# Table products of split queries, the division of local attention, and counts in bf16, in a two-layer attention kernel with an expert layer

## The chip, the cores and the metric

The kernel runs on one core of one Trainium2 chip. The metric is the time of one execution on the device in microseconds, over the whole program. Engines are called TensorE (PE, with PEld for its loads of stationary operands), VectorE (DVE), ScalarE (ACT), GpSimd (POOL) and SyncE (SP), whose queue issues most DMAs.

## The reference

Input x is 8 images of 16x16 positions with 192 channels, in float32. Cut to what matters:

```python
# layer 0: windowed attention (12 heads of 16, windows of 14x14, padded), then an MLP
qkv = win(layer_norm(x)) @ qkv_w + qkv_b
attn = (q * 0.25) @ k.T
rel_h = einsum('bhwc,hkc->bhwk', q, Rh)      # Rh, Rw: tables of relative positions
rel_w = einsum('bhwc,wkc->bhwk', q, Rw)
attn = softmax(attn + rel_h[..., :, None] + rel_w[..., None, :])
x = x + (attn @ v) @ proj_w + proj_b
x = x + gelu(layer_norm(x) @ fc1_w + fc1_b) @ fc2_w + fc2_b
# layer 1: causal attention over the 256 positions (12 heads of 16), then 8 experts, top 2
t = t + causal_attention(ln(t)) @ lin_w.T + lin_b
gates = softmax(ln(t) @ gate_w + gate_b); the two largest, divided by their sum
t = t + sum over the two experts of gate * (gelu(ln(t) @ w1[e] + b1[e]) @ w2[e] + b2[e])
```

## The kernel before

**Stages.** The 8 images go through a pipeline. `run(step)` makes nine steps; in step s, image s is in stage a, image s-1 in b, s-2 in c and s-3 in d (`step(a, b, c, d)`, written out by hand for every engine). Stage a: layer norm, queries, keys and values of local attention (`transpose_a`, `q_a`, `k_a`, `v_a_main`, `v_a_out`) and the table products (`rel_rows`, `rel_columns`). Stage b: local attention itself (`max_a`, `row_a`, `attend_a`, `output_a`) and the MLP (`transpose_m`, `fc1`, `fc2`). Stage c: the second attention (`q_b` to `v_b_all`, `max_b_of`, `row_b`, `attend_b`, `output_b`). Stage d: routing (`gate`, `choose`, `count`, `locate`, `scatter`). After the loop, `last` finishes the second attention of the last image between the first of 39 expert tiles (`tile_transpose`, `tile_fc1`, `tile_fc2`), and a last pass adds the experts' rows. What order instructions have on an engine is that of the code; engines wait for one another by semaphores that count.

**Local attention with tables.** A head pair's queries lie on 128 partitions, head e of the pair on a slot of 64 rows: each slot has 32 rows in which a channel's high and low part go, then 28 rows for the position terms, one for the maximum and three for masks. For each of 16 rows and 16 columns of the image one product, `positions` (L1815 to L1819), multiplies a table `rel_w[:, table, :]` (128 stationary columns) with the queries `s_q` of the 16 positions in that row or column, for six pairs at once: 96 moving columns. The results of the rows are copied by ScalarE (`rel_rows`, L860) into `rel_sum`, those of the columns added by VectorE (`rel_columns`, L1231). Both operands are float32. `s_q` gets its 16 query rows of a slot by a DMA from `staged_a` (L388), and its constant rows once by a DMA.

Four positions make a block of a bank (BANK_A, two halves in turn), so an image has four row blocks and four column blocks; each column block waits for the addition or copy two blocks earlier. After the last, `split_odd`, `split` and `split_even` cut `rel_sum` into a float32r high part and the rest, and the next step's first maxima product waits for that.

**Division.** The value products of four heads (a group, `values_a`) land in BANK_Z with the sum of a head's exponentials in the row behind its 16 channels. `normalise_a` (L1278 to L1284) copies that row over the other rows of its 32 with a shuffle, takes the reciprocal of 128x256 numbers, and multiplies three pieces into `o_a`, from the order of windows into the order of the image. The next group's value products wait for the semaphore `ot_a` of the last piece. The second attention does it otherwise (`normalise_b`, L1344 to L1352): transpose of 32x32 blocks, so that a head's sum lies beside its channels, a reciprocal of 8 columns, one product, and a transpose back.

**Rows of maxima.** Each attention takes the maxima of all heads first, transposes them on TensorE (`row_a`, `row_b`, L2018), has ScalarE copy them, and a DMA puts them into the queries as one row (L401, L422). `attend_a` and `attend_b` wait for that DMA (`row_in_a`, `row_in_b`).

**Counts.** `count` (L2079 to L2081) multiplies a triangle of ones and a square of ones with the choices of the tokens, in float32, with up to 16 moving columns.

## Time and profile before

| | us |
|---|---|
| median of 3 runs | 863.15 |
| the three runs | 858.99, 863.15, 865.65 |
| the profiled execution | 858.26 |
| its span (first to last instruction) | 856.4 |
| mean granted clock of TensorE | 0.933 of full |

The profile is of one execution. Its times are in microseconds from the start of the span. Busy time of TensorE is that of pipelined products with modelled ends, so it is no measure of its peak. The clock is granted at one of two levels, 1.00 being 2.4 GHz and 0.5 being 1.2 GHz; a stretch shows the mean.

### The profile page before, as it was taken

To read this page: it belongs to the slowest core of one execution; us is meant where nothing else is said; L and a number is where in the kernel's file an instruction comes from. 1 tells how busy PE (TensorE), PEld (TensorE's weight loads), DVE (VectorE), ACT (ScalarE), POOL (GpSimd) and SP (SyncE) were. 2 spreads that over 40 slices of the span, in tenths; PEclk is the share of its full clock that TensorE was granted. 3 is DMA by queue.
4 is the path that set the end of the run, shared out by engine and by line. 5 is a ranking of instruction groups with operands and counts; after the bars stand their busy time and mean duration, and the time that the engine had idled before them with its cause. 6 is when DMAs were issued, how large, how long until landed. Compare 5 with 4: busy or idle time off the path is not lost.

```text
span 856.4 us, 15650 instructions
## 1 busy us (share of the span) xinstructions
PE 737.3 (86%) x5694; PEld 647.3 (76%) x5694; DVE 448.4 (52%) x1073; ACT 333.1 (39%) x724; POOL 156.1 (18%) x306
## 2 busy tenths in 40 slices
PE   4688889989989988998998998878688999999990
PEld 3558778868868867886886887757577999999990
DVE  4355656857667683575767768353534222222213
ACT  6124354333433523344353452423273444444430
POOL 5010000121030220113103022012204121211210
PEclk9999999999999996899999998579798999999995
DMA  6702944931030212203012021955304111111117
GB/s 223 176 11 72 250 108 130 226 94 43 24 89 6 67 38 56 57 11 94 23 46 77 19 57 38 238 151 159 111 7 121 43 39 42 44 42 39 43 34 225
DMA packets 62049, 72.18 MB, mean 84 GB/s; under 512 B 6370, under 2 KB 52286, under 8 KB 61846
## 3 DMA queue, kind: packets, MB, share of 16 engines
q1 hardware_dynamic: 58566, 64.17, 27.7%
q0 software_dynamic: 3408, 7.02, 2.7%
q8 instruction: 47, 0.77, 0.4%
q14 instruction: 28, 0.23, 0.1%
HBM read 27.26 MB, written 23.17 MB: 59 GB/s over the span
## 4 chain that ended last, share of the span: by engine, by line
PE 73%; DVE 9%; DMA 6%; issue 5%; ACT 4%; SPq 1%; POOL 1%; another core or an unknown queue 1%; DVEq 0%; POOLq 0%; ACTq 0%
PE ps L2129 8%; PE ps L1819 7%; PE ps L2112 6%; PE ps L2113 6%; PE ps L1777 5%; PE ps L1778 5%; PE ps L1971 4%; PE ps L1944 4%; PE ps L1995 3%; PE ps L1896 3%; PE ps L1910 3%; DVE max_rows_a L1260 2%; PE ps L2034 2%; DMA q_rows_a<-max_at 2%; PE ps L1863 2%
## 5 line engine op out<-in xcount | busy, mean ns | idle before, releaser
L2112 PE MATMUL ps<-rows_t,w_tile 97*128 97x128 f32 x468 | 91.4, 276 | 3.3 <-DVE rows_t L1488 3.3
L2113 PE MATMUL ps<-rows_t,w_tile 96*128 96x128 f32 x468 | 90.5, 274 | 0.0
L2129 PE MATMUL ps<-w_exp,hid_t 128*128 x468 | 84.2, 331 | 2.3 <-DVE y_out L1496 1.4
L1479 DVE COPY w_tile<-w_exp 96x768 f32 x39 | 21.7, 556 | 120.3 <-PE ps L2113 102.1
L1328 DVE TENSOR_REDUCE max_b<-ps 128x3 f32<-128x384 f32 x96 | 48.6, 549 | 68.9 <-PE ps L2012 67.9
L1819 PE MATMUL ps<-s_q,rel_w 128*128 128x96 f32 x512 | 79.5, 314 | 3.0 <-DMA s_q<-staged_a 1.2
L2129 PEld LDWEIGHTS ps<-w_exp,hid_t 128*128 128x128 f32 x468 | 76.4, 193 | 3.5 <-issue 3.5
L1819 PEld LDWEIGHTS ps<-s_q,rel_w 128*128 128x128 f32 x512 | 74.3, 203 | 5.1 <-issue 2.7
L2112 PEld LDWEIGHTS ps<-rows_t,w_tile 97*128 97x128 f32 x468 | 72.4, 191 | 5.2 <-DVE rows_t L1488 5.1
L881 ACT ACTIVATE probs_a<-ps 98x392 f32<-98x392 f32 x96 | 47.9, 499 | 70.1 <-PE ps L1899 68.3
L2113 PEld LDWEIGHTS ps<-rows_t,w_tile 96*128 96x128 f32 x468 | 70.8, 191 | 0.0
L682 POOL DMA_INDIRECT y_dram<-y_out,tile_x x39 | 37.4, 958 | 167.9 <-DVE y_out L1496 167.4
L917 ACT ACTIVATE probs_b<-ps 128x384 f32<-128x384 f32 x96 | 42.2, 488 | 34.3 <-PE ps L2025 33.2
L1896 PE MATMUL ps<-q_rows_a,ks_a 128*98 128x196 f32 x192 | 44.1, 316 | 9.8 <-DMA q_rows_a<-max_at 7.4
L1260 DVE TENSOR_REDUCE max_rows_a<-ps 98x4 f32<-98x784 f32 x48 | 46.3, 965 | 11.6 <-PE ps L1863 9.9
L951 ACT ACTIVATE b_gate<-b,tile_x 128x192 f32 x39 | 17.7, 455 | 82.5 <-DVE y_out L1496 75.2
L941 ACT ACTIVATE hid_t<-ps 128x384 f32<-128x384 f32 x78 | 37.3, 482 | 25.5 <-PE ps L2113 23.5
L1863 PE MATMUL ps<-ks_a,q_rows_a 128*98 128x196 f32 x192 | 31.2, 287 | 18.2 <-DVE max_rows_a L1260 9.6
L1995 PE MATMUL ps<-mask_q,ident 128*128 128x256 bf16 x96 | 30.7, 320 | 18.4 <-issue 11.5
L615 POOL TENSOR_TENSOR x_2b<-x,b_fc 128x384 f32<-128x384 f32 x8 | 8.0, 1003 | 209.0 <-DVE x L1292 209.0
L1863 PEld LDWEIGHTS ps<-ks_a,q_rows_a 128*98 128x98 f32 x192 | 22.9, 176 | 26.7 <-DVE max_rows_a L1260 15.7
L1280 DVE RECIPROCAL den<-den 128x256 f32<-128x256 f32 x24 | 42.1, 1753 | 0.8
(229 smaller groups left out, 1633.0 us busy)
## 6 DMA issues: line engine op xcount, KB each, us to landing
xs_dram<-blank SPq DMA_DIRECT2D x32, 388.0 KB, 8.6
w_exp<-in_e_w SPq DMA_DIRECT2D x16, 576.0 KB
ks_a<-staged_a SPq DMA_DIRECT2D x32, 192.0 KB
qs_b<-staged_b SPq DMA_DIRECT2D x32, 192.0 KB
ks_b<-staged_b SPq DMA_DIRECT2D x32, 192.0 KB
tile_x<-xs_dram SPq DMA_DIRECT2D x39, 97.0 KB
w_exp<-y_dram SPq DMA_DIRECT2D x8, 384.0 KB, 6.7
rel_w<-in_rel_tables SPq DMA_DIRECT2D x1, 1792.0 KB, 9.6
```

Source lines behind the costliest of these rows:

```text
L881: ac.activation(probs_a[0:HALF, p % 3, e, 0:2 * WIN], BANK_W[0:HALF, e, 0:2 * WIN], ACT.Exp)
L1260: dv.tensor_reduce(max_rows_a[0:HALF, 0:2, 2 * p:2 * p + 2].rearrange("p q e -> p e q"), BANK_W[0:HALF, :, 0:2 * WIN].rearrange("p e (q k) ...
L1328: ins = dv.tensor_reduce(max_b3[:, h, :], BANK_C[:, h % 3, 0:384].rearrange("p (a k) -> p a k", a=3), AX.X, ALU.max, negate=True).then_inc ...
L1777: pe.matmul(dst, w[0:DC + ones, 0, cols], x[0:DC + ones, 0, :], start=True, stop=False)
L1778: return pe.matmul(dst, w[0:DC, 1, cols], x[0:DC, 1, :], start=False, stop=True)
L1819: return pe.matmul(dst, rel_w[:, table, :], toks, start=True, stop=True)
L1863: ins = pe.matmul(BANK_W[0:HALF, e, q * WIN:(q + 1) * WIN], qs_a[:, 2 * p + e, q * HALF:(q + 1) * HALF], ks_a[:, 2 * p + e, 0:WIN], start= ...
L1896: pe.matmul(bank[0:HALF, k * WIN:(k + 1) * WIN], ks_a[:, h, k * HALF:(k + 1) * HALF], qs_a[:, h, 0:WIN], start=True, stop=True)
L1995: pe.matmul(bank.rearrange("p (a k) -> p a k", a=2)[:, :, 0:P], ident16[:, :], mask[:, :, :], start=True, stop=False, skip_group_check=True)
L2112: pe.matmul(dst, w1_tile[t % 2][:, 0, cols], rows_t[t % 2][:, 0, :], start=True, stop=False)
L2113: ins = pe.matmul(dst, w1_tile[t % 2][0:DC, 1, cols], rows_t[t % 2][0:DC, 1, :], start=False, stop=True)
L2129: ins = pe.matmul(TILE_Y[:, 0:D], hid_t[t % 2][:, f, :], w_exp[:, bass.ds(e, 1), 2 * MLP + f * D:2 * MLP + (f + 1) * D].rearrange("p e d - ...
```

## The change

- **Table products.** `s_q` and `rel_w` are float32r. Of a slot's 32 rows before the position columns only 16 were used for the queries; now a slot of 64 holds the high part of the queries, their low part, the high part again, and the constants (in rows 48 to 63). The tables have their high part twice, then their low part. So one float32r product per position gives high x high + low x high + high x low. The number of positions and the 96 moving columns stay; each was two float32 instructions and is one now.
- For that VectorE takes the low part of the queries (`low_queries_a`), and SP issues six DMAs an image into `s_q` in place of two. In the first step the raw tables come by 16 DMAs into `probs_a` and `hid`, ScalarE (`tables_set`) and VectorE (`low_tables`) round them and VectorE subtracts the low part, and POOL fills the constant rows of `s_q` (`query_rows_set`).
- **Division of local attention** by blocks transposed, as in the second attention, into `hid`; POOL copies the result into `o_a` (`place_a`). The next group's value products wait for the first transpose (`dn_a`, and `dn_b` in the second attention).
- **Counts** with bf16 operands.
- The hand-written orders of all engines are permuted.

```diff
-            s_q = sb("s_q", [P, PAIRS, TOK])
+            s_q = sb("s_q", [P, PAIRS, TOK], F32R)
...
-        rel_loads = ((s_q[:, :, :], a["slot_rows_q"].unsqueeze(1).to_broadcast([P, PAIRS, TOK])),
-                     (rel_w[:, :, :], a["rel_tables"]))
+        rel_loads = [(q_rows_in, a["slot_rows_q"])]
+        for s in (0, SLOT):
+            for part, tables in zip(raw_tables, TABLES):
+                rel_loads += [(part[s + HD * n:s + HD * (n + 1)], a["rel_tables"][r:r + HD, tables])
+                              for n, r in enumerate((s, s, s, s + SLOT - HD))]
...
             def queries_in_a(i):
...
+                for s in (0, SLOT):
+                    for r in (s, s + 2 * HD):
+                        sp.dma_start(s_q[r:r + HD, :, :].bitcast(F32), staged_a[:, s // SLOT, :]).then_inc(q_in_a, 16)
+                sp.wait_ge(ql_a, i + 1)
+                for s in (0, SLOT):
+                    sp.dma_start(s_q[s + HD:s + 2 * HD, :, :].bitcast(F32), low_q[:, s // SLOT, :]).then_inc(q_in_a, 16)
...
+            def query_rows_set(i):
+                if i == 0:
+                    gp.wait_ge(rel_in, REL_IN)
+                    gp.tensor_copy(s_q[:, :, :], q_rows_in.unsqueeze(1).to_broadcast([P, PAIRS, TOK])
+                                   ).then_inc(constants_set, 1)
...
+            def place_a(g):
+                def go(i):
+                    gp.wait_ge(back_a, GROUPS * i + g + 1)
+                    hold(gp)
+                    for dst, src in zip(window_pieces(yx(o_a[:, g:g + 1, :])), win_order(hid[:, 2 * g + 1:2 * g + 2, :])):
+                        ins = gp.tensor_copy(dst[:, 0], src[:, 0])
+                    ins.then_inc(ot_a, 1)
...
+            def tables_set(i):
+                if i == 0:
+                    ac.wait_ge(rel_in, REL_IN)
+                    ac.copy(rel_w[:, TABLES[0], :], raw_tables[0]).then_inc(rel_set, 1)
...
+            def low_tables(i):
+                if i == 0:
+                    dv.wait_ge(rel_in, REL_IN)
+                    dv.tensor_copy(rel_w[:, TABLES[1], :], raw_tables[1]).then_inc(rel_set, 1)
+                    dv.wait_ge(rel_set, 2)
+                    for s in (0, SLOT):
+                        rows = slice(s + REL, s + REL + HD)
+                        for n, tables in enumerate(TABLES):
+                            cols = slice(s, s + REL + 2 * WS)
+                            part = rel_w[rows, tables, cols]
+                            ins = dv.tensor_tensor(part, raw_tables[n][rows, :, cols],
+                                                   part.bitcast(F32), ALU.subtract)
+                    ins.then_inc(rel_set, 1)
...
+            def low_queries_a(i):
+                dv.wait_ge(qh_a, i + 1)
...
+                dv.tensor_tensor(flat(low_q).bitcast(F32R), BANK_A[0:DC, 1], flat(staged_a[:, 0:2, :]),
+                                 ALU.subtract).then_inc(ql_a, 1)
...
-                    dv.stream_shuffle(den[:, :], src, [HD] * 32).then_inc(dn_a, 1)
+                    dv.transpose(turned, BANK_Z[:, 0:TOK]).then_inc(dn_a, 1)
                     dv.wait_ge(dn_a, done)
-                    dv.reciprocal(den[:, :], den[:, :]).then_inc(rc_a, 1)
+                    dv.reciprocal(sums, blocks[:, :, HD]).then_inc(rc_a, 1)
...
+                    dv.tensor_tensor(blocks[:, :, 0:HD + 1], blocks[:, :, 0:HD + 1],
+                                     sums.unsqueeze(2).to_broadcast([P, TOK // 32, HD + 1]), ALU.mult).then_inc(ml_a, 1)
+                    dv.wait_ge(ml_a, done)
+                    dv.transpose(hid[:, 2 * g + 1, :], turned).then_inc(back_a, 1)
...
             def v_a_main(i):
                 pe.wait_ge(qh_a, i + 1)
+                pe.wait_ge(ql_a, i + 1)
...
-                            pe.wait_ge(ot_a, GROUPS * i + p // 2 - 1)
+                            pe.wait_ge(dn_a, GROUPS * i + p // 2 - 1)
...
-                pe.matmul(counts, before[:, :], both[:, :, :].rearrange("p t e -> p (t e)"), start=True, stop=False)
+                pe.matmul(counts, before16[:, :], both[:, :, :].rearrange("p t e -> p (t e)"), start=True, stop=False)
```

The order of TensorE around the second attention's row of maxima, in a steady step. L1944 is the output product of local attention, L1819 the table products, L2018 and L2019 the transposes of the maxima, L1995 the first product that waits for their DMA. Before (the row block ahead of the output is the third of the image):

```order
L1819 MATMUL ps<-s_q,rel_w 128x96 x8
L1944 MATMUL ps<-w_out_a,o_a 128x192 x6
L1819 MATMUL ps<-s_q,rel_w 128x96 x4
L2018 MATMUL ps<-ident,max_b 12x128
L2019 MATMUL ps<-ident,max_b 12x128
L1819 MATMUL ps<-s_q,rel_w 128x96 x8
L1995 MATMUL ps<-mask_k,ident 128x2x128
```

The same place of TensorE in the changed kernel, where L1898 are the table products, L2023 the output, L2097 and L2098 the transposes and L2074 the product that waits:

```order
L1898 MATMUL ps<-s_q,rel_w 128x96 x4
L2023 MATMUL ps<-w_out_a,o_a 128x192 x6
L2097 MATMUL ps<-ident,max_b 12x128
L2098 MATMUL ps<-ident,max_b 12x128
L1898 MATMUL ps<-s_q,rel_w 128x96 x16
L2074 MATMUL ps<-mask_k,ident 128x2x128
```

Two row blocks moved from ahead of the transposes to behind them, so four blocks (16 products) now stand between the transposes and the product that waits.

VectorE in the first step, from the constants to the first addition of a column block. Before:

```order
L1187 CAST mask_q<-probs_a 128x256
L1188 CAST mask_k<-probs_a 128x256
L1222 SCALAR_TENSOR_TENSOR staged_a<-ps,staged_a 96x512
L1231 TENSOR_TENSOR rel_sum<-ps,rel_sum 128x4x96 x4
L1247 CAST q_rows_a<-rel_sum 64x6x196
```

VectorE in the changed kernel, at the same place (L1270 and L1277 make the tables, L1286 the low queries, L1291 the low keys, L1300 the additions):

```order
L1233 CAST mask_q<-probs_a 128x256
L1234 CAST mask_k<-probs_a 128x256
L1270 CAST rel_w<-hid 128x1536
L1277 TENSOR_TENSOR rel_w<-probs_a,rel_w 16x16x60
L1277 TENSOR_TENSOR rel_w<-hid,rel_w 16x12x60
L1277 TENSOR_TENSOR rel_w<-probs_a,rel_w 16x16x60
L1277 TENSOR_TENSOR rel_w<-hid,rel_w 16x12x60
L1286 TENSOR_TENSOR rel_sum<-ps,staged_a 96x512
L1291 SCALAR_TENSOR_TENSOR staged_a<-ps,staged_a 96x512
L1300 TENSOR_TENSOR rel_sum<-ps,rel_sum 128x4x96 x4
```

Five instructions for the tables and one for the low queries stand ahead of the low keys now. The order also moves, among others: statistics of the next image ahead of the first reduction of a step; `k_b` behind `count`; `max_b_of(7)` ahead of `attend_a(6)`; `v_a_main` behind `attend_a(5)`; the last column block ahead of `fc1(1)`.

## Rows read from the trace of the kernel before

**Rows 1.** The page: busy time by engine, and the table products' group.

```profile
PE 737.3 (86%) x5694; PEld 647.3 (76%) x5694; DVE 448.4 (52%) x1073; ACT 333.1 (39%) x724; POOL 156.1 (18%) x306
...
L1819 PE MATMUL ps<-s_q,rel_w 128*128 128x96 f32 x512 | 79.5, 314 | 3.0 <-DMA s_q<-staged_a 1.2
```

**Rows 2.** Stretches: us, busy PE, PEld, DVE, ACT, POOL, clock, DMA share, GB/s.

```profile
308.30:386.50 78.20, 70.81 (x525) 59.58 (x524) 46.87 (x114) 28.68 (x69) 13.70 (x31) 0.87 0.16 44
386.50:455.00 68.50, 61.67 (x524) 52.57 (x523) 46.57 (x113) 28.24 (x69) 13.69 (x31) 1.00 0.18 51
523.50:596.50 73.00, 59.34 (x416) 49.55 (x414) 34.81 (x91) 24.67 (x58) 11.62 (x25) 0.73 0.60 172
```

**Rows 3.** The chain of waits, 386.5 to 455 us: start, us, what.

```profile
419.88 1.76 PE ps L1819 x16
...
424.48 0.11 PE ps L2018
...
424.70 2.63 PE ps L1819 x16
427.33 0.23 issue
...
434.61 1.35 PE ps L1819 x8
```

**Rows 4.** The same chain, score products of one head of local attention.

```profile
406.05 0.16 PE ps L1899 x2
406.21 0.24 PE ps L1896 x2
```

**Rows 5.** The row of maxima: SP's issue (timeline), a DMA of another step (chain).

```profile
425.12 0.80 SPq L422 DMA_DIRECT2D qs_b<-max_bt  x1
...
138.88 2.21 DMA qs_b<-max_bt
```

**Rows 6.** Groups by line and shape, VectorE and POOL: busy us, mean ns, idle before.

```profile
L1260 DVE TENSOR_REDUCE max_rows_a<-ps 98x4 f32<-98x784 f32 x48 | 46.3, 965 | 11.6 <-PE ps L1863 9.9
L1280 DVE RECIPROCAL den<-den 128x256 f32<-128x256 f32 x24 | 42.1, 1753 | 0.8
L1238 DVE TENSOR_TENSOR q_rows_a<-rel_sum,q_rows_a 64x1176 fp32r<-64x1176 f32 x16 | 22.0, 1378 | 0.4
...
L1344 DVE STREAM_TRANSPOSE o_heads<-ps 128x256 f32<-128x256 f32 x24 | 10.8, 449 | 34.7 <-PE ps L2034 33.9
...
L1348 DVE TENSOR_TENSOR o_heads<-o_heads,sums_b 128x136 f32<-128x136 f32 x24 | 7.2, 302 | 0.8
...
L1316 DVE TENSOR_TENSOR staged_b<-ps,staged_b 96x512 fp32r<-96x512 f32 x8 | 5.4, 673 | 3.3 <-ACT staged_b L897 3.3
...
L1346 DVE RECIPROCAL sums_b<-o_heads 128x8 f32<-128x8 f32 x24 | 4.9, 203 | 0.8
...
L606 POOL COPY x_tw<-xt_a 97x196 f32<-97x196 f32 x16 | 7.3, 456 | 15.5 <-ACT xt_a L793 15.5
```

**Rows 7.** Chain of 518 to 665 us, and TensorE's waits of 518 to 600 us.

```profile
554.46 0.46 DVE den L1278
...
556.73 0.56 DVE o_a L1284 x3
...
595.97 0.61 PE ps L2079 x2
...
PE ps L1995 <- DMA qs_b<-max_bt: 2.7, 1, 2.7
```

**Rows 8.** Timeline of the first step.

```profile
10.85 4.71 ACT L827 CAST ks_a<-probs_a 32x5424 fp32r<-32x5424 f32 x1
...
18.74 0.58 ACT L837 ACTIVATE staged_a<-ps 96x512 f32<-96x512 f32 x1
...
19.38 0.96 PE L1782 MATMUL ps<-w_qkv_a,x_tw 97*98 97x192 f32 x2
...
24.96 10.84 PE L1819 MATMUL ps<-s_q,rel_w 128*128 128x96 f32 x64 [1.24 <-DMA s_q<-staged_a]
```

More of the change, by code:

```diff
@@ L142, in layers @@
         hot = sb("hot", [P, 2, 2, NE])
-        both = sb("both", [P, 2, NE])
-        seen = sb("seen", [P, 2, NE])
+        both = sb("both", [P, 2, NE], BF16)
+        seen = sb("seen", [P, 2, NE], BF16)
         sums = sb("sums", [P, 2, 4])
@@ L1381, in route_constants @@
                     dv.wait_ge(route_in, ROUTE_IN)
+                    after(dv.tensor_copy(before16[:, :], before[:, :]))
                     after(dv.tensor_reduce(lane[:, :], before[:, :], AX.X, ALU.add))
@@ L2244, in step @@
                     fc1(1)(i)
+                for i in c:
+                    output_b(i)
+                for i in b:
                     fc1(2)(i)
```

255 lines of the change are left out of this document (139 added, 116 removed).

## The prediction

> **What bounds the kernel now.** I read the page first. TensorE is busy for 737.3 of 856.4 us [rows 1]; no other engine comes near. A busy TensorE need not be one at its peak, so the second view was the stretches by step. In the loop of nine steps up to four images are at work at once. A steady step (386.5 to 455.0) is 68.5 us long, TensorE busy for 61.67 of it, VectorE for 46.57 [rows 2]. Third came the chain of waits inside that step, to see whether a product taken from TensorE shortens the step or only uncovers something. It is nearly all TensorE; so it shortens, unless the product was covering a wait. Hence I looked at what stands beside the table products in that chain [rows 3]. They are its largest single item: 512 instructions (two for each of 256 float32 products), 79.5 us [rows 1].
>
> **The table products.** A block is four products of 96 moving columns; an image has four row blocks and four column blocks. In the chain two row blocks take 1.76 us, so 0.88 each, and two column blocks, whose moving operand is read with a stride, 2.63, a single one 1.35 [rows 3]. An image costs 4 x 0.88 + 4 x 1.33 = 8.8 us. Now each product is one float32r instruction instead of two float32 ones. No row shows it with 96 columns. The nearest are the float32r score products: one head's four, with 98, 98, 128 and 128 stationary columns, take 0.24 + 0.16 = 0.40 us [rows 4], though the two wide ones move only 60 columns. That looks like the cost of loading the stationary operand: 452 columns in 0.40 us, 0.113 us for 128, 0.45 us a block, row or column. Bounds: below, the 0.16 us pair alone, 0.32 a block; above, one of today's two instructions, 0.44 for a row block and 0.67 for a column block. I take 0.45, because a head's four stand back to back as the table products will. Saved per image: 8.8 - 8 x 0.45 = 5.2 us (4.4 to 6.2), 42 us in eight images if all of it counted.
>
> The Trainium skill, FP8 and Floating Point Precision, section TensorE Precision Notes, gives full float32 four passes through the array. By an estimate from that page alone the new product costs a quarter of the old, 0.22 us a row block and 0.33 a column block, and an image saves 6.6 us. The trace speaks against it: a product of 60 columns in rows 4 does not shrink with what it moves. The sum does not use it.
>
> **What the table products cover.** Here I part with the full 42 us. In the second attention the row of maxima leaves by a DMA and comes back. From its first transpose at 424.48 to the issue at 425.12 is 0.64 us, and the DMA takes 2.21 [rows 3, 5], some 2.9 to 3.0 in all. Beside it lay two column blocks (2.63) and 0.23 of waiting [rows 3]. Now four blocks do, 4 x 0.45 = 1.8 us, so 1.2 are idle. Second, the first row block waits for a copy of values that ScalarE can start only when the last value products of the image before are done; fewer maxima products stand between now, and I charge 0.4 us. Third, the attention phases are paced by ScalarE's exponentials: a column block between them hides 0.2 us less than it saves.
> A steady step: 5.2 - 1.2 - 0.4 + 0.2 (the old wait, which is inside the 3.0) - 0.2 = 3.6, and the new order takes away one 0.3 us wait on the exponentials of local attention: 3.9.
>
> **The first 15 us of a step** are VectorE's: six pairs of reductions (the larger 0.965 each [rows 6]), two normalisations and the routing choice, back to back. The change permutes them (statistics of the next image go ahead of the first reduction, to cover POOL's power). Walking through both orders I get the same within 0.3 us. The bf16 counts take less of TensorE there, where it is not what is waited for. Six steps: 6 x 3.9 = 23.4 us.
>
> **Local attention's division.** Before: shuffle 0.46, reciprocal of 256 columns 1.753, three products 0.56 together, and the next image group's value products wait for the end [rows 6, 7]. Now: two transposes of 0.449, a reciprocal of 8 columns 0.203, one product 0.302 [rows 6], 1.4 us instead of 2.8, 24 times: VectorE is relieved of 33 us. POOL gets three copies a group: 0.456 for 196 columns [rows 6] and about as much again for the two short ones. The result is in place after 1.4 + 0.95 + hand-overs = 2.6 us, against 2.9: no change. But the next value products now wait for the first transpose only, 0.5 us. In a steady step that wait lies under maxima products. In step 8 it is on the chain once, 554.46 to 557.3 [rows 7]: 2.5 us saved there, and about 1 us in step 1, which has no second attention to cover it.
> The Trainium skill, GPSIMD Engine Reference, section Key points, says that POOL shares its SBUF interfaces with VectorE and contends when VectorE has two SBUF inputs. No row here isolates that. If each copy group held VectorE up for its own 0.95 us it would be 3 us a step of an engine that idles for 22 [rows 2], hardly anything in the sum.
>
> **Low parts of the queries.** VectorE gets a subtraction of 96x512 per image, 0.673 us by L1316 [rows 6], in a stretch where it idles. SP issues six DMAs instead of two per image; they have some 10 us before the first table product, and behind them on the queue stand DMAs not wanted before the next step.
>
> **Start.** Here it costs. Before, the table products run from 24.96 for 10.84 us [rows 8]. Now ScalarE, which begins its first staging at 18.74, casts 2048 columns of tables behind two stagings of 0.6 us. At 4.71 us for 5424 [rows 8] that is 1.8 us, to 21.8. VectorE waits for it, then subtracts twice 960 and twice 720 elements; at 1.378 for 1176 [rows 6] 3.9 us (overhead counted), to 25.7, then the low queries to 26.4. The value products wait for these: at 19.38 before, 26.4 now. The table products came 5.6 us behind them, so they start at 32.0. They take not 10.84 but about 5.8 us (4.7 at the upper clock, 6.9 at the lower), paced by ScalarE's copies and VectorE's additions. End 37.8 instead of 35.8: 2.0 us lost (0 to 5).
>
> **Rest.** Step 1 has the 5.2 of the tables, less 1.7 that now waits for POOL and VectorE ahead of the MLP's first layer, plus 1 for the division: 4.5. After the loop two counts stand on the chain, the first pair of instructions 0.61 us [rows 7], the three pairs 1.5; three bf16 ones take about 0.3: 2.3 us for both. The 39 expert tiles are untouched.
>
> **Sum**, against the profiled execution of 858.3 us (span 856.4): 23.4 + 4.5 + 2.5 + 2.3 - 2.0 = 30.7, so 827.6. The median of the runs shown, 863.15, is 4.9 above the profiled one. How such a difference arises is to be seen in two stretches with the same work: 78.2 us at a granted clock of 0.87, 68.5 at 1.00 [rows 2]. I take 829.
>
> **The rivals.**
> 1. *The clock falls more often.* In the stretch 523.5 to 596.5, without table products, TensorE waits 2.7 us for that same row DMA and the mean granted clock is 0.73 [rows 2, 7]. The change thins the stretch around the row DMA in six more steps. If in half of them the clock drops to 1.2 GHz for some 7 us, half of it TensorE's, each costs 3 us or more, about 10 together: 839. Against it: dense products follow at once. The Trainium skill, TensorE: Matmul & The Clock Gate, section HAM oscillation, says that gaps between groups of products let the clock fall so that the next group starts slow; by that rule this rival is the usual course. Chance 0.20 (837 to 850).
> 2. *The saving counts in full*: 42 us of tables, 5 of division and counts, a start that costs nothing: 858.3 - 47 = 811. For it: TensorE is busy for 90% of a step. Against it: the row DMA's own 2.2 us. Chance 0.17 (809 to 822).
> 3. *Slower.* The clock falls at the row DMA in every steady step and, as in the stretch at 0.87, comes back so late that each loses 9.7 us: 58 us against 31 saved, 886. It decides from 5 us lost per step on. Against it: the step at 1.00 has waits of about 2 us as well. Chance 0.03.
> 4. *It does little*: a float32r product of 96 columns costs as much as two float32 ones, or is not what limits; the division and counts alone give 854 to 858. Rows 4 speak against it. Chance 0.03.
>
> **How the numbers follow.** Forecast 0.57, at 823 to 837. Low end 810, from rival 2; high end 844, from rival 1 with the start at its worst. About 1% (8.6 us) is what a measurement of this kernel can tell from no change. Faster by more: 0.57 + 0.20 + 0.17 = 0.94; within: 0.03; slower: 0.03.
>
> **What would show it.** Table products: 256 instructions, 0.45 us a block, columns like rows. Steady step 64.6 us at full clock. A new wait of the second attention's mask product for the row DMA, about 1.2 us in each of six steps. First table product at about 32, the first step's maxima 2 us later. VectorE busy for some 25 us less; POOL for 23 more. If column blocks stand at 0.67, a step is 0.9 us longer. My account is wrong if the row DMA is not waited for, or if steps at full clock are over 66.5 us.

## The result, and the profile after

| | before | after |
|---|---|---|
| median | 861.07 us (4 runs, 850.67 to 865.65) | 823.9 us (4 runs, 821.69 to 827.58) |
| the profiled execution | 858.26 | 827.58 |
| its span | 856.4 | 824.9 |
| mean granted clock | 0.933 | 0.937 |
| ratio after/before | | 0.9643, 95% interval 0.9585 to 0.97 |

Here and below a median is over all executions, and a ratio leaves out those that took over 1.5% longer than the fastest of the same kernel.

The forecast was 829; the two profiled executions differ by 30.7 us, the very sum that was forecast. That looks better than it is. The parts of the sum came out otherwise, and the experiments show that its largest part was put down to half of its cause: to the shorter table products, without the new division that lets them count.

The page after, busy time by engine and two groups (line engine op, out<-in, shape xcount | busy, mean ns | idle before), against [rows 1]:

```profile
PE 696.6 (84%) x5412; PEld 605.8 (73%) x5412; DVE 428.1 (52%) x1039; ACT 333.3 (40%) x725; POOL 176.6 (21%) x379
...
L1898 PE MATMUL ps<-s_q,rel_w 128*128 128x96 f32 x256 | 43.3, 311 | 8.2 <-ACT v_a L897 4.0
...
L636 POOL COPY o_a<-hid 128x196 f32<-128x196 f32 (+2 forms) x72 | 15.5, 256 | 149.7 <-DVE hid L1354 149.7
```

The table products are 256 and not 512. TensorE is busy 41 us less, VectorE 20 less, GpSimd 20 more, as expected to within 5 us.

The chain of waits of a steady step after, around the second attention's row of maxima (start, us, what), against [rows 3]:

```profile
403.33 0.11 PE ps L2097
...
403.58 0.37 ACT max_bt L956
...
403.97 2.41 DMA qs_b<-max_bt
...
406.43 0.28 PE ps L2074
...
408.32 0.45 PE ps L1898 x4
...
410.72 0.50 ACT probs_b L962
...
411.77 0.50 ACT probs_b L962
...
414.09 0.88 ACT probs_b L962 x2
...
417.85 0.40 PE ps L1898 x4
```

A block costs 0.45 us, columns like rows (a single one 0.40). The table products are gone from the chain beside the DMA: all four blocks end sooner than it does. From the first transpose (403.33) to the mask product (406.43) it is 3.1 us, the 3.0 of the forecast.

The stretches, in the columns of [rows 2]: the first step, step 1, and two steady steps, the slowest and a usual one; then the steady step that follows, at full clock, in its parts, up to the first maxima product of the second attention (L2074), up to the transposes (L2097), and from the mask product to the end:

```profile
0.00:46.39 46.39, 20.10 (x64) 14.69 (x64) 22.77 (x36) 19.09 (x21) 13.19 (x25) 1.00 0.83 178
46.39:102.60 56.21, 47.88 (x336) 39.11 (x336) 28.62 (x64) 19.83 (x49) 6.10 (x21) 0.88 0.42 102
...
166.28:234.87 68.59, 61.95 (x488) 52.03 (x489) 43.58 (x109) 28.20 (x70) 16.17 (x40) 0.90 0.32 81
...
299.67:364.36 64.69, 57.97 (x488) 48.68 (x489) 43.44 (x109) 28.12 (x70) 16.04 (x40) 0.97 0.21 60
364.36:386.69 22.33, 17.94 (x115) 13.77 (x116) 15.18 (x41) 7.39 (x19) 3.95 (x14) 1.00 0.25 72
386.69:403.16 16.47, 15.96 (x196) 14.05 (x197) 11.25 (x27) 7.34 (x23) 5.12 (x18) 1.00 0.16 44
406.42:428.34 21.92, 20.11 (x160) 17.34 (x161) 14.81 (x36) 11.73 (x25) 4.88 (x5) 1.00 0.22 65
```

The same parts of the step of [rows 2, second row] in the kernel before:

```profile
381.38:405.01 23.63, 18.29 (x117) 14.30 (x118) 14.88 (x41) 8.82 (x22) 8.30 (x24) 1.00 0.30 85
405.01:424.32 19.31, 18.82 (x221) 16.97 (x221) 15.36 (x34) 6.94 (x21) 0.02 (x1) 1.00 0.01 2
427.56:450.03 22.47, 21.69 (x169) 18.74 (x169) 14.38 (x34) 11.76 (x25) 2.44 (x4) 1.00 0.18 51
```

I call these parts A (first maxima), B (local attention with the second attention's maxima), T (transposes to mask product) and C (second attention, MLP). The first maxima product of each step marks its start: 41.66, 95.62, 163.59 ... 518.25 before; 46.39, 102.60, 166.28 ... 492.42 after. Where the 31.5 us of span are, and where the forecast had them:

| | before | after | gain | forecast |
|---|---|---|---|---|
| first step | 41.66 | 46.39 | -4.7 | -2.0 |
| step 1 | 53.96 | 56.21 | -2.2 | +4.5 |
| steps 2 to 7 | 422.6 | 389.8 | +32.8 | +23.4 |
| rest | 338.15 | 332.48 | +5.7 | +4.8 |

A steady step at full clock goes from 68.65 to 63.98, 4.7 us. In parts: A -1.3, B -2.8, T none, C -0.6. Six times that is 28.0 of the 32.8. The rest is the clock's, in these two executions: the kernel before lost some 9.5 us in one fall (its stretch at 0.87 [rows 2]), and the changed kernel 4.6 in the step from 166.28, with the clock at half for 13.7 us in three falls. That these are draws of an execution is likely and not shown: e9 below, nearly the kernel before, has no such fall there, but one of 34 us in its step 1.

### The profile page after: what moved, and what is told of

Its sections match the earlier page's. It is cut to its first block, busy times and chain, and to the rows that moved or that the text cites. A ratio compares the mean times of both kernels' runs of the same rounds, so it can differ in the third digit from the quotient of the medians.

```text
span 824.9 us, 15205 instructions
## 1 busy us (share of the span) xinstructions
PE 696.6 (84%) x5412; PEld 605.8 (73%) x5412; DVE 428.1 (52%) x1039; ACT 333.3 (40%) x725; POOL 176.6 (21%) x379
## 4 chain that ended last, share of the span: by engine, by line
PE 70%; DVE 10%; DMA 7%; issue 4%; ACT 4%; SPq 3%; POOL 1%; DVEq 0%; POOLq 0%; ACTq 0%
PE ps L2208 9%; PE ps L2192 6%; PE ps L2191 6%; PE ps L1855 6%; PE ps L1856 5%; PE ps L2023 4%; PE ps L2050 4%; PE ps L2074 4%; PE ps L1975 3%; DVE max_rows_a L1329 3%; PE ps L1898 3%; PE ps L1989 3%; PE ps L1942 2%; PE ps L2113 2%; DMA q_rows_a<-max_at 2%
## 5 line engine op out<-in xcount | busy, mean ns | idle before, releaser
L1549 DVE COPY w_tile<-w_exp 96x768 f32 x39 | 21.7, 556 | 116.4 <-PE ps L2192 105.5
L962 ACT ACTIVATE probs_b<-ps 128x384 f32<-128x384 f32 x96 | 42.6, 489 | 26.2 <-PE ps L2104 21.6
L1898 PE MATMUL ps<-s_q,rel_w 128*128 128x96 f32 x256 | 43.3, 311 | 8.2 <-ACT v_a L897 4.0
L1942 PE MATMUL ps<-ks_a,q_rows_a 128*98 128x196 f32 x192 | 34.1, 305 | 18.9 <-DVE max_rows_a L1329 10.5
L986 ACT ACTIVATE hid_t<-ps 128x384 f32<-128x384 f32 x78 | 37.5, 482 | 30.2 <-PE ps L2192 30.2
L1975 PE MATMUL ps<-q_rows_a,ks_a 128*98 128x196 f32 x192 | 41.6, 301 | 7.3 <-DMA q_rows_a<-max_at 6.6
L636 POOL COPY o_a<-hid 128x196 f32<-128x196 f32 (+2 forms) x72 | 15.5, 256 | 149.7 <-DVE hid L1354 149.7
L1898 PEld LDWEIGHTS ps<-s_q,rel_w 128*128 128x128 f32 x256 | 38.1, 217 | 12.5 <-issue 6.5
L1942 PEld LDWEIGHTS ps<-ks_a,q_rows_a 128*98 128x98 f32 x192 | 24.9, 186 | 28.8 <-DVE max_rows_a L1329 16.8
L2104 PE MATMUL ps<-qs_b,ks_b 128*128 128x256 f32 x192 | 39.5, 310 | 0.0
L2074 PE MATMUL ps<-mask_q,ident 128*128 128x256 bf16 x96 | 29.3, 305 | 11.9 <-DMA ks_b<-staged_b 7.2
```

Source lines behind the costliest of these rows:

```text
L962: ac.activation(probs_b[:, p % 3, e, :], BANK_C[:, e, 0:384], ACT.Exp).then_inc(pr_b, 1)
L1898: return pe.matmul(dst, rel_w[:, table, :], toks, start=True, stop=True)
L1942: ins = pe.matmul(BANK_W[0:HALF, e, q * WIN:(q + 1) * WIN], qs_a[:, 2 * p + e, q * HALF:(q + 1) * HALF], ks_a[:, 2 * p + e, 0:WIN], start= ...
L1975: pe.matmul(bank[0:HALF, k * WIN:(k + 1) * WIN], ks_a[:, h, k * HALF:(k + 1) * HALF], qs_a[:, h, 0:WIN], start=True, stop=True)
L2074: pe.matmul(bank.rearrange("p (a k) -> p a k", a=2)[:, :, 0:P], ident16[:, :], mask[:, :, :], start=True, stop=False, skip_group_check=True)
```

## The experiments

Since the kernel has three intertwined edits (tables, division, order), I first undid one or two at a time. All twelve, with the ratio to the kernel before on the same chip; the clock is that of the profiled execution:

| run | median us | ratio, 95% | clock |
|---|---|---|---|
| e1 new order and division, float32 tables | 844.88 | 0.9846 (0.9748 to 0.9944) | 0.946 |
| e2 new order and tables, old division | 860.14 | 1.0011 (0.9971 to 1.005) | 0.913 |
| e3 new order, both old | 867.73 | 1.0138 (1.0052 to 1.0224) | 0.944 |
| e4 old order, both new | 840.19 | 0.9772 (0.9688 to 0.9855) | 0.919 |
| e5 old order, new division | 855.21 | 0.997 (0.9917 to 1.0023) | 0.942 |
| e6 old order, new tables | 867.31 | 1.015 (1.0071 to 1.023) | 0.905 |
| e7 as e4, row's wait filled | 842.81 | 0.9878 (0.9774 to 0.9981) | 0.938 |
| e8 after, start and step 1 | 816.93 | 0.9533 (0.9451 to 0.9614) | 0.930 |
| e9 before, scatters late | 856.58 | 0.9971 (0.9915 to 1.0028) | 0.921 |
| e10 after, four edits | 822.07 | 0.9596 (0.9497 to 0.9695) | 0.945 |
| after, again | 820.75 | 0.9561 (0.947 to 0.9652) | 0.949 |
| e11 as e10, one more wait filled | 826.14 | 0.952 (0.9419 to 0.9621) | 0.931 |

**e1: the table products back in float32.**

```diff
-                return pe.matmul(dst, rel_w[:, table, :], toks, start=True, stop=True)
+                return pe.matmul(dst, rel_w[:, table, :].bitcast(F32), toks.bitcast(F32), start=True, stop=True)
```

> The changed kernel with only the table products back in plain float32 (two instructions each; layout, low parts, division, order as changed). Theory A (the tables' saving is partly lost to the row's DMA): a block costs 0.88 us for rows and 1.33 for columns, so four blocks stand as 4.4 us beside the 3.0 us DMA and the wait for it vanishes. Undoing costs 5.2 - 1.2 - 0.2 = 3.8 us in each of six steady steps, 3.5 in step 1 and 2.6 at the start, 29 in all: about 853 us. Theory B (the saving counts in full): 42 us, about 866. Theory C (little of the gain is the tables'): below 840. Steady step at full clock: A 67.8 us, B 69.2.

844.88 us, ratio 0.9846. The changed kernel has 0.9643, and 0.9561 when it ran again, so the tables are worth 2.0 to 2.9% here, 17 to 25 us. That excludes theory B's 42; theory A's 29 lies at the edge of it. The steady step is 67.35, with one short fall of the clock, nearest to theory A.

**e2: the old division in the new order.**

```diff
-                    dv.transpose(turned, BANK_Z[:, 0:TOK]).then_inc(dn_a, 1)
...
+                    dv.stream_shuffle(den, src, [HD] * 32).then_inc(dn_a, 1)
+                    dv.wait_ge(dn_a, done)
+                    dv.reciprocal(den, den).then_inc(rc_a, 1)
...
-                            pe.wait_ge(dn_a, GROUPS * i + p // 2 - 1)
+                            pe.wait_ge(ot_a, GROUPS * i + p // 2 - 1)
```

> The changed kernel with local attention divided as before: shuffle, reciprocal of 256 columns and three products on VectorE, no copies by POOL, and the next group's value products wait for the last product. Theory A (as predicted): only steps without cover feel it, 2.5 us in step 8 and 1 in step 1, 3.5 in all, about 827.5 us; steady steps within 0.3 us of 64.0. Theory B: VectorE's 33 us less of work also shortened steady steps, since the first stretch of a step is its own; then each steady step grows by 1 us or more and the total is over 833. Theory C (POOL's copies contend with VectorE or come late): 824 or less.

860.14 us, ratio 1.0011: the whole gain is gone. Theory A falls by a factor of ten. Of the 36.7 us of span between this run and the changed kernel, 22.7 are in steps 2 to 7, 7.6 in step 1 and 6.8 after the loop; the first step is 0.4 shorter. Part of it is the clock: in steps 2 to 7 it was at half for 44 us in this run and for 27 after the change. The chain of waits of a steady step of this run (start, us, what) runs through VectorE where that of the kernel before is nearly all TensorE:

```profile
339.96 0.45 issue
340.40 0.46 DVE hid L1341 x2
...
340.88 1.77 DVE hid L1343
...
344.80 0.48 DVE max_b L1391
...
345.75 1.76 DVE hid L1343
...
347.53 0.55 DVE o_a L1347 x3
```

L1343 is the reciprocal of 256 columns (its buffer lies in `hid` here), L1391 a maximum of the second attention, for which the next maxima product waits. Part B of that step:

```profile
337.18:356.44 19.26, 16.30 (x197) 14.05 (x197) 15.24 (x33) 7.35 (x23) 0.00 (x0) 1.00 0.12 33
```

TensorE has 16.3 us of work in B, but B takes 19.26, since VectorE has 15.24 and must go to and fro with it.

**e3: both back, the new order alone.** The edits of e1 and e2 together.

> The changed kernel with both float32 tables and the old division: what is left of the change is the order, the bf16 counts, the low queries and the start. By theory A the two undone parts add up: 29 + 3.5, about 856.5 us, that is 0 to 5 us under the kernel before. If they don't add (old division hides in what the slow tables leave idle), below 853; if the order is worth something by itself, also below 853 with steady steps at full clock of under 67.5 us.

867.73 us: slower than the kernel before, which no theory had. The parts do not add up. In the new order the division is worth 2.9% with old tables (e3 to e1) and 3.7% with new ones (e2 to after; 4.5% with the repeated run).

**e4: the old orders, with all new parts.** The `step` and `last` functions of every engine as before; `place_a` behind `to_windows`, the low parts ahead of `low_keys_a`.

> The changed kernel with all hand-written orders as before, the new pieces put at the nearest place. Theory A: two row blocks now stand ahead of the transposes of the maxima, so only 0.9 us of table products lie beside the 3.0 us of the row's DMA and not 1.8; the second attention's mask product waits about 2.1 us in a steady step, 0.9 more, and the 0.3 us wait on exponentials is back: 1.2 a step, seven steps, about 832 us. Theory B (the order is worth nothing, another wait takes its place): 822 to 826. Theory C (the order carries much of the gain): over 836, with the difference in the first 15 us of a step or in the maxima products of the second attention.

840.19 us: theory C by its total. The order is worth 1.3% once both parts are there (2.1% by the repeated run). B is 17.5 and not 16.5. Much of the rest is the clock, at half for 48 us in steps 2 to 7 against 27. These steps take from 65.3 us at a clock of 0.97 to 68.2 at 0.92:

```profile
374.81:440.11 65.30, 57.71 (x488) 48.24 (x489) 42.98 (x109) 28.32 (x70) 15.65 (x40) 0.97 0.23 59
...
240.42:308.63 68.21, 59.98 (x488) 50.23 (x489) 43.02 (x109) 28.45 (x70) 15.68 (x40) 0.92 0.22 57
```

TensorE's longest waits in the second of them (engine, line, what for: us, times, longest):

```profile
PE ps L2065 <- DMA qs_b<-max_bt: 2.3, 1, 2.3
```

In this step the clock was at half for 6.8 us from 284.3, about 44 us into the step, where this wait stands. All six of these steps have a fall there, of 6.8 us in two and of 3.4 in four.

**e5 and e6: one part alone, in the old order.** The edits of e1 and of e2, each applied to e4.

> Old orders, new division, counts and low queries, but float32 tables: the change without its fast table products and without its new order. Theory A (VectorE's work hides in the old order): only 2.5 us in step 8, 1 in step 1 and 2.3 for the counts come off, less what the start costs, so 856 to 861 us, and steady steps at full clock are 68.5 us as before. Theory V (VectorE sets the pace in the stretch of local attention, as in the run with the old division in the new order): steady steps get shorter by 1 us or more without any faster table product, total under 853.

> Old orders, old division, and the new table products: the tables alone. Against 840.2 us of the run with the old orders and both new parts. Theory A (the old division hides in the old order, it was only exposed by the new one): 2.5 + 1 more, 842 to 846 us. Theory V (once the table products are short, VectorE's three divisions of 2.8 us stand on the chain in either order): 2 to 4 us a step more, 852 to 865, so that the tables alone would give hardly anything.

e5 took 855.21, ratio 0.997, theory A by its steps: alone, in the old order, the new division gives next to nothing in a steady step (68.40 against 68.65), as the prediction had it. e6 took 867.31, ratio 1.015, above even theory V: the edit of the tables alone makes the kernel slower. Both runs, like e3 and e4, also carry what the new tables cost at the start: the first maxima come at 49.6 in e5 and 46.5 in e6, and at 41.66 in the kernel before. So neither ratio is the worth of a steady step. Two steps of e6, and its chain where the second attention's maxima begin and where they end:

```profile
457.00:525.73 68.73, 59.34 (x489) 49.18 (x489) 47.23 (x115) 28.36 (x71) 13.72 (x31) 0.95 0.20 53
385.15:457.00 71.85, 63.24 (x488) 52.48 (x489) 47.29 (x115) 28.65 (x70) 13.72 (x31) 0.88 0.19 54
```

```profile
336.03 2.78 issue
...
353.60 0.44 DVE hid L1339
...
354.07 1.76 DVE hid L1341
...
355.86 0.56 DVE o_a L1345 x3
...
356.46 1.57 PE ps L2009 x8
```

The local output (L2009) now waits for the last division: the row blocks ahead of it used to cover that. The 2.78 us stand ahead of the product that waits in the code for the keys' DMA (`k_in_b`); the profile names no releaser for it. And the clock was lower in every run of this kernel, 0.902 on the mean. Behind the wait for the keys (some 25 us into a step) and behind that for the row (some 47) it fell, and four of its five steady steps had it at half for 10 to 17 us.

The four parts of a steady step in each of the eight kernels, from the starts of the same four products (L1942, L2074, L2097, L2074 of the kernel after) in one of its steps least disturbed, and how long the clock was at half in it:

| order | division | tables | A | B | T | C | step | at half |
|---|---|---|---|---|---|---|---|---|
| old | old | old (before) | 23.6 | 19.3 | 3.2 | 22.5 | 68.6 | 0 |
| old | new | old (e5) | 23.5 | 19.3 | 3.1 | 22.5 | 68.4 | 3.4 |
| old | old | new (e6) | 24.9 | 17.9 | 3.1 | 22.9 | 68.7 | 6.8 |
| old | new | new (e4) | 22.1 | 17.5 | 3.4 | 22.4 | 65.3 | 3.4 |
| new | old | old (e3) | 22.3 | 19.7 | 4.8 | 23.2 | 70.0 | 0 |
| new | new | old (e1) | 22.3 | 17.3 | 4.8 | 22.9 | 67.4 | 3.4 |
| new | old | new (e2) | 23.1 | 19.3 | 3.1 | 22.6 | 68.0 | 6.8 |
| new | new | new (after) | 22.3 | 16.5 | 3.3 | 21.9 | 64.0 | 0 |

Column by column. In the new order B falls only with the new division (19.7 to 17.3, 19.3 to 16.5); in the old order it falls with the tables, by 1.5 with the old division and 1.9 with the new. T is the DMA's 3.1 to 3.4 wherever the table products behind the transposes are shorter than it, and 4.8 where four blocks of them are float32.

C seems to move little with the tables, but a fall of the clock hides it. In steps of the same traces whose C has none it is 22.5 in the kernel before and in e5, 21.7 in e7 (e4 with products added), 22.9 in e1 and e3, 21.6 in e2 and 21.9 after. So the new tables take 0.8 to 1.3 off C, and the new order puts 0.4 on it. In the same way A is 22.3 in e2 and 24.0 in e6.

**e7: the row's wait filled with work.** Sixteen dummy products ahead of `attend_b(0)`, in e4.

```diff
                 for i in c:
+                    cover(16)
                     attend_b(0)(i)
```

> The run with the old orders and both new parts (840.2 us), and 16 dummy bf16 products of 256 columns between the last table product and the mask product that waits for the row's DMA (1.7 us at full clock, inside a wait of 2.3 to 3.2). Their results are not used. Theory K (the wait makes the clock fall, 6.8 and 3.4 us at half in five of seven steps, some 2.5 us lost each): the falls about 43 us into a step vanish, steps of 68 become 65.5, total 828 to 832. Theory N (the clock falls for another reason, or the loss is the wait itself): the falls stay and the total is 839 to 843.

842.81 us: theory N by its total. But the fall at 44 us was gone in four of five steady steps. The one some 4 us into a step, 3.4 us long in e4, was 6.8 in two of these steps (from 241.8 and from 310.1), which take 69.0 and 68.7 us.

The falls were not removed, but in steps 2 to 7 they add up to 31 us and not 48, and the six steps still take 405.2 us against 402.4. The dummy products run past the DMA's end in part (T 3.5 to 4.9 us in this run), so the run is no clean measure of the clock alone.

**e8: the start, and a wait in step 1.** Step 1's chain after the change: TensorE waits for the second layer norm, which the slower table products used to cover, and then runs the MLP's first products at half clock (0.85 us a pair):

```profile
82.81 1.00 POOL x_2b L646
...
84.13 0.71 POOL rstd_m L613
...
85.59 0.66 PE ps L1830 x4
...
86.27 1.02 ACT xt_m L832 x2
...
88.56 0.85 PE ps L1856 x2
```

```diff
+                    if i == 0:
+                        pe.wait_ge(dve_set, 1)
+                        cover(16)
                     rel_rows(0)(i)
...
+                    if i == 0:
+                        cover(24)
                     transpose_m(i)
...
+                    low_queries_a(0)
+                    low_keys_a(0)
                     dv.wait_ge(masks_loaded, 16)
```

> The changed kernel with two edits. In the first step VectorE takes the low parts of queries and keys ahead of masks and tables, so the value products don't wait for the tables, and 16 dummy products stand ahead of the first table product; in step 1, 24 dummy products (2.6 us) stand where TensorE waits 2.1 us for the second layer norm. If the start was lost to the queue on VectorE: first maxima at 42.5 to 44 us and not 46.4. If step 1 was lost to the clock at half from 86.7 to 97.0: step 1 is 52 us and not 56.2. Both: 824 - 3 - 4, about 817. If the clock falls all the same, step 1 stays at 56 and the total is 821; if the start was bound by the DMAs of the queries into their rows, it gains under 1 us.

The total, 816.93, is the 817 of the first theory, but its parts are not. Step 1 is 53.65 and not 56.21, its clock 0.96 and not 0.88. That doesn't show that the dummy products did it: the changed kernel run again (below), without them, had a step 1 of 52.92 at 0.97. The start gained 0.4 us: the table products now wait for the DMA of the low queries (timeline of the first step):

```profile
32.80 7.34 PE L1901 MATMUL ps<-s_q,rel_w 128*128 128x96 f32 x32 [5.41 <-DMA s_q<-rel_sum]
```

Eight copies of blank rows (L391) also stood ahead of the next keys on SyncE's queue, up to 1.25 us each, and step 1 ended 3.0 us late for these keys.

**e9: the scatters late, in the kernel before.**

```diff
-                for i in d:
-                    scatter(0)(i)
-                    scatter(1)(i)
                 for i in b:
                     blank_rows(i)
                     add_b2(i)
                     rstds("m")(i)
                 for i in d:
+                    scatter(0)(i)
+                    scatter(1)(i)
                     scatter(2)(i)
```

> The kernel before with one edit: GpSimd's first two scatters of a step stand behind the statistics of the second layer norm, together with the other two, and not beside the keys' DMA of the second attention. Theory S (the scatters slow that DMA, from issue to the mask product 6.9 us before, 5.9 in the runs where they come later): the wait of the first mask product of the maxima goes from 1.9 to 0.9 us in each of five steps, about 5 us off: 853 to 857 where the kernel before has 861. Theory O (it is where the keys' copies stand in the order of ScalarE and VectorE, or the query rows behind them on the queue): the wait stays at 1.9 and the time at 859 to 863.

856.58 us, ratio 0.9971: by the total no difference that can be told. The profiled execution took 865.37 us, with a long fall of the clock in step 1, but the step below is at full clock. By its parts theory S holds and is worth nothing: in the step at 386.96 A is 22.5 and not 23.6, since the maxima product comes 5.7 us after the keys' DMA is issued (403.75) and not 6.9 (398.16 to 405.01), but C is 23.3 and not 22.5:

```profile
386.96:455.35 68.39, 62.04 (x524) 52.72 (x524) 46.71 (x114) 28.24 (x71) 13.56 (x31) 1.00 0.18 51
```

C has new waits on exponentials and on a division of the second attention there; by what path the later scatters cause them I did not find.

**e10, and the changed kernel again.**

```diff
-                    gp.wait_ge(rel_in, REL_IN)
+                    gp.wait_ge(q_rows_loaded, 16)
...
                     next_x(i)
-                    fill(0)(i)
-                    fill(1)(i)
                 for i in a:
                     keys_in_a(i)
+                    pads_in(i)
                 for i in b:
+                    fill(0)(i)
+                    fill(1)(i)
                     fill(2)(i)
```

> The changed kernel with four edits: dummy products in step 1 as in the run before; in the first step the low parts of queries and keys ahead of tables and masks; the constant rows of the queries wait for their own DMA, and the pads' keys are moved into place behind the queries' and keys' DMAs; the blank rows (fills) of a step stand behind the keys' DMAs on SyncE's queue. If the start was bound by the DMA of the low queries (5.4 us of wait for it, ended at 32.8), the first table product starts at about 28.5, when VectorE's tables are ready, and the first maxima are at 42 and not 46. If step 1 waited 3.0 us for keys that stood behind eight fills, it is 51 us and not 53.7. Total 817 - 4 - 3, about 810 us. If the first step is bound elsewhere, 814 to 818.

> The changed kernel itself beside these, to compare them on one chip in the same minutes: every theory expects 0.964 of the kernel before, within its interval (0.9585 to 0.97), and steady steps of 64 to 65 us.

The start and step 1 did about what was expected (39.7 and 52.1 us, against 42 and 51; the same stretches as above, of e10):

```profile
0.00:39.67 39.67, 20.12 (x64) 14.67 (x64) 22.53 (x36) 19.00 (x21) 13.15 (x25) 1.00 0.90 199
39.67:91.72 52.05, 45.28 (x360) 36.84 (x360) 28.67 (x64) 19.77 (x49) 6.13 (x21) 0.97 0.40 99
```

The first table product starts at 26.45 and the first maxima come at 39.67, 6.7 us sooner than after the change and 2.0 sooner than before it. But the total, 822.07, missed both forecasts (810, or 814 to 818), and the ratios of e10 and of the changed kernel beside it, 0.9596 and 0.9561, can't be told apart. The second lies a little under the interval that was expected for it (0.9585 to 0.97), with an interval of its own that reaches into it. Their profiled spans are 811.5 and 814.8. Steps 2 to 7 of e10 are 390.0 us and of the repeated run 385.7: one step of e10 had the clock at half for 10 us (68.32), and two of the repeated run's took only 63.84 and 64.06. The changed kernel again had a step 1 of 52.92 and not 56.21, after a first step of 47.42 and not 46.39. So up to 3.3 of the 6.7 us missed in step 1 were a draw of that execution; of both steps together 2.3.

**e11: one more wait filled**, ten dummy products ahead of `transpose_b` in every step, added to e10.

> The run with the four edits, and ten dummy products of 256 columns (1.1 us at full clock) ahead of the second attention's transposes in every step, inside the 1.4 us that TensorE waits there for VectorE's normalised rows. Theory K (the wait opens the way for the fall of the clock some 4 us into a step, 3.4 us at half, about 0.7 us lost in each): these falls vanish and steady steps are 63.9 to 64.1 us and not 64.7; ratio to the kernel before 0.945 to 0.952. Theory M (as with the products laid into the row's wait: a fall that is filled in one place comes in another, or these products do not count): steps stay at 64.7 or grow by up to 0.5, and the ratio is 0.953 to 0.962.

Theory M by its steps, 64.7 to 65.0. The ratio, 0.952, is the upper end of theory K's, with an interval that covers both. The falls some 4 us into a step were gone, and each steady step had one of 3.4 us at 43 us instead (280.1, 345.0, 409.8, 474.7). The profiled execution, 829.44 us, also had a fall of 37.5 us in step 2, which the steps given here leave out. TensorE did ten products more and the mean clock of a step stayed 0.97:

```profile
302.12:366.89 64.77, 59.11 (x498) 49.53 (x499) 43.43 (x109) 28.07 (x70) 16.09 (x40) 0.97 0.21 60
```

Thus none of e8, e10 and e11 is shown to beat the changed kernel; all beat the kernel before. The bf16 counts were never undone by themselves.

## Why the prediction was right, and where it was not

**The block** (0.45 us): right, 0.45 for rows and for columns. The estimate by four passes, from the page FP8 and Floating Point Precision of the Trainium skill, section TensorE Precision Notes (0.22 and 0.33 us), is not borne out.

**The row's DMA** (3.0 us, 1.2 of it idle): the length is right. T is 3.1 to 3.4 in the table wherever the blocks are shorter than it. The idle time is not all where the forecast looked for it. At the mask product the trace has 0.18 us of waiting for the DMA (at 406.43; under 0.1 in the other steps), and 0.44 stand between the first block and the other three, for a copy of ScalarE (at 404.37). But the DMA still lands last, so it sets T.

**"The full 42 us don't count"**: right. Rival 2 did not come (811 forecast, 823.9 measured; e1 gives the tables 17 to 25 us in the new order). Rival 4 and rival 3 did not happen.

**The steady step** (64.6 forecast; 64.7 with one short fall, 63.98 with none): near as a sum, by errors of opposite sign: the full-clock step gained 4.7 us and not 3.9.
- "The first 15 us of a step ... the same within 0.3 us": with all of A up to the second attention's first maxima product, 1.3 us less. Before, TensorE waited 1.9 at the product that waits for the keys' DMA, 0.3 after. It is not VectorE's time, and not the new order's alone. e1, e2, e3 and after have A at 22.3, but so, nearly, have e9 (22.5), in which only two scatters moved, and e4 (22.1), whose old order has GpSimd's new copies (`place_a`) ahead of the scatters. In the kernel before and in e6 (24.0) two scatters stand right behind the keys' DMA. So what counts is whether they do. (In e5, where none do either, A has a fall of the clock in every step.)
- "a column block between them hides 0.2 us less than it saves": 1.2 less. The two column blocks in C lost 0.9 each, and C is 0.6 shorter. By the table 0.4 of the 1.2 is the new order's, which makes C 22.9 with float32 tables; the rest, 0.8, is this term. The chain shows the exponentials (L962) at three places in the middle of that attention, where it was all TensorE before; attention up to its last value products takes 9.5 us (406.43 to 415.92) and took 9.2 with the slow block in it (427.56 to 436.74). Of the terms of a steady step, that of the first 15 us (1.3 for 0) and this one are furthest off.

**"In a steady step that wait lies under maxima products"**, so the division counts for 3.5 us in all: this is the step that failed. It holds for the division alone in the old order (e5). It does not hold for the kernel that was to be predicted: there the division decides over 3.7% of the time (e2), as much as the whole change gives, and 2.8 us of each steady step are lost in B. The rows of the kernel before show a part of why. In its part B VectorE is busy 15.36 of 19.31 us, with waits of 0.7, 0.6 and 0.8 for TensorE's products between:

```profile
407.86 0.45 DVE L1278 STREAM_SHUFFLE den<-ps 128x256 f32<-128x256 f32 x1
408.34 1.75 DVE L1280 RECIPROCAL den<-den 128x256 f32<-128x256 f32 x1
...
410.60 1.01 DVE L1328 TENSOR_REDUCE max_b<-ps 128x3 f32<-128x384 f32 x2
...
422.44 0.17 DVE L1332 TENSOR_TENSOR max_b<-max_b 128x12 f32<-128x12 f32 x1
```

The maxima are complete at 422.61 and the transposes start at 424.32: 1.7 us of slack. The change takes 1.7 us from the four row blocks of B and moves two of the remaining ones behind the transposes, 0.9 more: 2.6 us, more than the slack. The old order bears that out: with short tables and the old division B becomes 17.85 (e6), 1.5 shorter. But the new order gets to 19.3 only (e2), and to 19.7 with float32 tables, where TensorE is busy for 17.2 of it (e3). So another 1.4 us or so lie in how the new order sends TensorE and VectorE to and fro; which move does it was not tried. I priced the division against the old TensorE and the tables against the old VectorE. "VectorE idles for 22 us a step" was true and no help, since 18 of them are not in B.

**The start** (-2.0 forecast, within 0 to 5): -4.7. The queue on VectorE was right, the landing was not: the tables were in at 20.3, the masks at 21.4 (before: 17.65), behind sixteen more DMAs. And the table products took 7.3 us, the upper bound of the forecast being 6.9. That is the pace of the lower level, though the profile has the granted clock at 1.00 there; the same products, just as long, stand in e8 with the clock recorded at half. e10 shows that 6.7 us can be had back by what waits for what and in which order.

**Step 1** (+4.5 forecast): -2.2, and +1.0 in the repeated run. "Less 1.7 that now waits for POOL and VectorE": it waits 2.1, and the clock fell behind it. That is rival 1's mechanism, at another place than the rival named; in the repeated run the fall there was 3.4 us and not 10. Rival 1 in its own place came true in three of six steps, with 3.4 us at half and some 0.7 us lost each (64.7 against 64.0), not 7 and 3; one of the three, from 166.28, has two more falls and lost 4.6 in all. In two steps of e4 and in most of e6 it came true in full. What the page TensorE: Matmul & The Clock Gate of the Trainium skill, section HAM oscillation, says of gaps agrees with step 1, with e4 and with e6, where falls follow the waits. Filling the waits did not settle it: in e7 and e11 the steps kept a fall at another place.

**The rest** (+4.8 forecast): +5.7, and +9.3 in the repeated run. It looks like the division's (`ot_a` waits are gone): in runs with the old division the rest takes 336.8 to 339.7 us (before, e2, e3, e6, e9), with the new one 328.8 to 334.3. How much of that is the clock, at half for 72 to 82 us there with the old division and for 55 to 72 with the new, stays open. The counts are now 4.2 us of products in all for 9.8, but of the 2.3 us forecast for them nothing shows: e3 has them and the old division and takes 338.2, as before.

**The equality of 30.7 and 30.7**: chance. The change lost 9.4 us more at the start and in step 1 than forecast, and gained 9.4 more in steps 2 to 7: 4.6 because a step gains 4.7 and not 3.9, and 4.8 because the clock cost the kernel before more than it cost the changed one.

## What to carry to other kernels

Before pricing an edit by the engine on the chain, take the stretch it stands in and add up what each other engine has to do in it, with its waits on the first. The distance to the second engine is about all that can be gained there (1.7 us of slack here, 1.5 gained by the tables alone in e6), and two edits that each give nothing or less alone (0.997 and 1.015 here) can give 2.3% together and 3.6% with the order fitted to them. Look also for costs that every such run carries: here what the new tables cost at the start is in all of them, so adding up the two ratios counts it twice. Undo parts from the final kernel and add them to the first one: only both directions show such a pair.

## What was not expected of the hardware

- Filling a wait did not rid a step of its fall of the clock. With dummy products in the wait at 44 us of a step the fall at 4 us stayed and was longer in two steps (e7); with them in the wait at 4 us, where e10 has its falls, five steps had theirs at 43 (e11). The changed kernel, with nothing filled, has them at either place, so it is not shown that the filling moves them. One fall of 3.4 us a step was usual in every version with steps below 65 us; it costs 0.1 to 0.8.
- The recorded clock can't be relied on at the start. The same 32 table products of the first step, in the changed kernel and in e8 (columns of [rows 2]):

```profile
33.19:40.53 7.34, 7.29 (x32) 6.97 (x32) 2.48 (x3) 1.91 (x4) 0.00 (x0) 1.00 0.81 197
32.80:40.14 7.34, 7.30 (x32) 6.97 (x32) 2.42 (x3) 1.92 (x4) 0.00 (x0) 0.50 0.98 219
```

- Short table products beside the long division were granted less clock: 0.902 on the mean of its runs in e6 and 0.918 in e2, against 0.945 in e1 and 0.940 in e3, so that part of what the shorter products gain is taken back. In steps 2 to 7 of e6 the clock was at half for 68 us. More waiting is not the whole account: in e3 TensorE waits for VectorE in B as it does in e2, yet has the clock in full in B in every step; what it lacks is the wait in T. Which wait decides was not tried.
- The DMA of the second attention's keys takes 5.3 us from its issue to the product that waits for it after the change and 5.7 in e9, but 6.9 and 7.7 with two scatters of GpSimd right behind its issue (before, e6). In e4 and e5, where no scatter stands there, it takes 5.8 and 5.9. e9 moves the scatters and nothing else.
